# VectorE's order of work in the first two steps of a gated attention and feed-forward kernel

## The reference, cut to what matters

```python
x = x + tanh(g_xattn) * attention(layernorm(x), ctx_768, Wq, Wk, Wv, Wo, bo)
x = x + tanh(g_ffn) * ffn(layernorm(x), w_gate, w_up, w_down)

def ffn(x, w_gate, w_up, w_down):
    g = bitlinear(x, w_gate)                      # 512 -> 2048
    u = bitlinear(x, w_up)                        # 512 -> 2048
    h = square(relu(g)) * u
    return bitlinear(h, w_down)                   # 2048 -> 512

def bitlinear(x, w):    # act_quant: round(x * 127 / max|x|) by row; weight_quant: round(w / mean|w|) in -1..1
    return act_quant(x) @ weight_quant(w).T
```

## Time and profile before

| | |
|---|---|
| median of 3 runs | 1192.84 us (1191.83 to 1193.57) |
| profiled execution | 1192.0 us, its span 1190.1 us |
| PE busy | 1169.0 us, 98% |
| DVE busy | 1035.5 us, 87% |
| ACT busy | 869.1 us, 73% |
| POOL busy | 307.0 us, 26% |
| DMA queue q1 | 47.4% of 16 engines' span |

### The profile page before, as it was taken

How to read it: one execution, slowest core, us unless ns; L and a number is a source line. 1 busy time by engine, 2 the same in 40 slices (tenths; PEclk the granted TensorE clock), 3 DMA queues, 4 the chain that set the end, 5 groups by cost and what they waited for, 6 DMA issues and landing times.

```text
span 1190.1 us, 18790 instructions
## 1 busy us (share of the span) xinstructions
PE 1169.0 (98%) x5802; PEld 742.8 (62%) x5867; DVE 1035.5 (87%) x2124; ACT 869.1 (73%) x929; POOL 307.0 (26%) x313
## 2 busy tenths in 40 slices
PE   9989899999999999999999999999999999999998
PEld 7656556666665666666566656656665666666554
DVE  4989898888988888888998888888899888988887
ACT  4877777776886777677877767776787777677764
POOL 3222222222442222222442222222244222222200
PEclk9999999999999999999999999999999999999999
DMA  9792654443444464444444464443443444444333
GB/s 354 263 302 67 156 142 109 98 108 93 101 115 102 114 167 110 97 103 107 101 99 98 114 178 112 98 107 94 101 114 97 104 97 110 96 99 112 84 65 75
DMA packets 286484, 144.69 MB, mean 122 GB/s; under 512 B 254586, under 2 KB 255226, under 8 KB 283889
## 3 DMA queue, kind: packets, MB, share of 16 engines
q1 hardware_dynamic: 286445, 144.32, 47.4%
q10 hardware_dynamic: 4, 0.00, 0.0%
HBM read 57.86 MB, written 24.35 MB: 69 GB/s over the span
## 4 chain that ended last, share of the span: by engine, by line
PE 88%; DVE 4%; DMA 3%; ACT 3%; issue 2%; SPq 0%; POOL 0%; ACTq 0%; DVEq 0%; POOLq 0%
PE gu_ps L1084 34%; PE o_ps L1048 18%; PE y_ps L1098 17%; PE s_ps L66 17%; DMA v_scr<-x 1%; DMA w_down<-in_wu_t 1%; DVE staged L1324 1%; PE gu_ps L1148 1%; DVE half_max L1330 1%; DMA a_scr<-a_spare 1%; DVE w_down L1484 0%; ACT staged L730 0%; ACT x L762 0%; PE y_ps L1141 0%; ACT k_pairs L864 0%
## 5 line engine op out<-in xcount | busy, mean ns | idle before, releaser
L1084 PE MATMUL gu_ps<-w_up,xq_t 128*128 128x512 bf16 x1024 | 241.9, 379 | 0.7 <-DVE staged L1324 0.7
L1084 PE MATMUL gu_ps<-w_gate,xq_t 128*128 128x512 bf16 x951 | 226.3, 379 | 8.6 <-DMA xq_t<-xq 3.9
L1098 PE MATMUL y_ps<-w_down,hq_t 128*128 128x512 bf16 x1008 | 227.8, 379 | 0.0
L1048 PE MATMUL o_ps<-v_sb,pt_high 128*128 128x512 f32 (+1 forms) x640 | 212.8, 413 | 1.1 <-DVE pt_low L1313 1.1
L1324 DVE TENSOR_TENSOR staged<-staged,gu_ps 128x1024 f32<-128x1024 f32 x128 | 155.6, 1215 | 53.8 <-ACT staged L784 53.8
L66 PE MATMUL s_ps<-a_sb,xf_high 128*128 128x308 f32 x1024 | 187.3, 305 | 0.0
L1084 PEld LDWEIGHTS gu_ps<-w_up,xq_t 128*128 128x128 bf16 x1024 | 99.5, 98 | 122.8 <-DVE staged L1324 2.6
L645 POOL TENSOR_TENSOR rstd<-var_eps,neg_half 128x1 f32<-128x1 f32 x128 | 96.6, 755 | 307.9 <-DVE var_eps L1289 275.2
L824 ACT ACTIVATE staged<-staged,h_scale 128x1024 f32<-128x1024 f32 x126 | 137.9, 1141 | 48.7 <-DVE h_scale L1344 48.7
L1098 PEld LDWEIGHTS y_ps<-w_down,hq_t 128*128 128x128 bf16 x1008 | 97.8, 97 | 119.7
L778 ACT ACTIVATE staged<-gu_ps 128x1024 f32<-128x1024 f32 x127 | 128.9, 1015 | 53.9 <-PE gu_ps L1084 53.5
(11 more groups left out here) (146 smaller groups left out, 1439.7 us busy)
## 6 DMA issues: line engine op xcount, KB each, us to landing
xf_sb<-in_x_feat SPq DMA_DIRECT2D x64, 256.0 KB, 2.7
x_sb<-in_x_tok SPq DMA_DIRECT2D x64, 256.0 KB, 2.8
y<-staged SPq DMA_DIRECT2D x63, 256.0 KB, 2.0
staged<-in_wg_t SPq DMA_DIRECT2D x4, 1024.0 KB, 9.8
staged<-in_wd_t SPq DMA_DIRECT2D x4, 1024.0 KB, 7.5
folded<-a_scr SPq DMA_DIRECT2D x3, 1232.0 KB, 5.3
v_scr<-x SPq DMA_DIRECT2D x12, 256.0 KB
folded<-v_scr SPq DMA_DIRECT2D x3, 1024.0 KB, 5.0
```

The costliest lines, as they stand in the source:

```text
L1048: last = nc.tensor.matmul(o_ps[:, :], pt[0:rows, P * c:P * (c + 1)], v_sb[0:rows, v, c, :], start=(c == 0 and pt is pt_high and v == 0), s ...
L1084: last = nc.tensor.matmul(target[:, q, :], xq_t[:, s.par(0), c, :], w[:, c, cols], start=(c == 0), stop=(c == DC - 1))
L1098: last = nc.tensor.matmul(y_ps[:, :], hq_t[:, c, :], w_down[:, c, :], start=(c == 0), stop=(c == FC - 1))
```

## The change

In step 0, DVE's top_half(0), the maximum of the first hidden half, moves from directly behind hidden_half(0) to behind shift_scores, so that the input chain of tile 1 comes first. Step 1 gets a written order of its own. In it hidden_half(1) moves up to directly behind unmark_input; shift_scores follows; input_stats of tile 4 moves from ahead of top_scores to behind shift_scores; then top_half(0); probs_low of tile 3 is taken over from the beginning of step 2; hidden_unit_scale, top_half(1) and hidden_scales follow; sum_probs of tile 4 moves from ahead of hidden_half(1) to the very end. No instruction is added or taken away, and no other engine's program changes.

```diff
                 def first_step(s):
                     input_stats(s, 3)
                     hidden_half(s, 0)
-                    top_half(s, 0)
                     add_attention(s, 1)
                     input_scale(s, 1)
                     top_scores(s, 3)
                     unmark_input(s, 1)
                     shift_scores(s, 3)
+                    top_half(s, 0)
                     ternary(2, 2, w_down)
                     hidden_half(s, 1)
                     probs_low(s, 2)
...
+                def second_step(s):
+                    unmark_hidden(s, -1)
+                    hidden_half(s, 0)
+                    add_attention(s, 1)
+                    input_scale(s, 1)
+                    top_scores(s, 3)
+                    unmark_input(s, 1)
+                    hidden_half(s, 1)
+                    shift_scores(s, 3)
+                    input_stats(s, 3)
+                    top_half(s, 0)
+                    probs_low(s, 2)
+                    hidden_unit_scale(s, 1)
+                    top_half(s, 1)
+                    hidden_scales(s)
+                    sum_probs(s, 3)
+
                 def step(s):
                     if s.opens(0):
                         first_step(s)
                         return
-                    if s.has(1) and not s.opens(1) and s.has(3):
+                    if s.opens(1):
+                        second_step(s)
+                        return
+                    if s.has(1) and not s.opens(2) and s.has(3):
                         probs_low(s, 1)
...
-                    if s.has(3) and not s.opens(1):
+                    if s.has(3):
                         input_stats(s, 3)
...
-                    if s.opens(1):
-                        input_stats(s, 3)
```

## The result

The changed kernel takes 1197.16 us in the median of 6 runs (1195.0 to 1198.25), the kernel before, beside it, 1192.49 (1191.31 to 1194.35, 6 runs). The ratio is 1.0037, 95% interval 1.0024 to 1.005: 4.7 us slower at the median. The forecast was 1195.8, slower by 2.9 us, with a range from 1193.0 to 1197.2: the measured median lies at its very end. The profiled execution took 1196.87 us, its span is 1194.9 (before 1192.0 and 1190.1).

A forecast was written before the change was run, and what follows sets the result against it. PE is busy 98% of the span, paced early by the DVE and ACT ring with 0.33 us slack. Ring 3.27 us late less slack makes PE 2.94 late: 1192.84 + 2.94 = 1195.8 us, range 1193.0 to 1197.2.

The forecast's parts named there:

- Step 0: Input chain of tile 1: 1.13 us earlier without top_half(0), but DVE and PE's up product gain only 0.6 us.
- Step 1, the visible gain: PE, tiles 2 and 3: earlier input chain brings attention of tile 3 to 121.7 from 126.03; PE gains 4.4 us.
- Step 1, the tail: Late sum_probs delays normalise and planes of tile 4, so mark_hidden of tile 1 starts at 128.43, not 125.16: 3.27 us.
- no collision: Bound for probs_low beside POOL's xf_low: 0 us added before hidden_unit_scale instead of 0.3; time 0.3 us lower.
- full exclusion: DVE and POOL exclude each other at probs_low: 0.8 us added before hidden_unit_scale instead of 0.3; time 0.5 us higher.
- The ring: DVE and ACT loop from h_scale through mark_hidden, relu, square, hidden_half(0) to next h_scale: 16.87 us, forecast 3.27 late.
- One sign: PE, step 3: new idle before attention of tile 4, which starts at about 146.2 instead of 143.22.
- the sum: Whole kernel: median 1192.84 plus PE's 2.94 us delay at attention of tile 4 gives 1195.8 us.
- Rival 4: SP's transposes of tile 4's planes and tile 1's hidden halves crowd; a transfer 2 us late gives 1197.3; chance 0.10.
- the likeliest case's own range: Ring 2.77 to 4.37 us late, so PE 2.4 to 4.0 later: 1195.3 to 1196.9 us; chance 0.65.
- Rivals 1 to 3: PE's gain stays, 1188.4 us (0.08); mark_hidden not held by planes, 1192.0 (0.10); lag mostly dissolves, 1193 (0.07).

The follow-up runs named there:

- e1_step0_only: Kernel before with step 0's edit alone (top_half(0) moved behind shift_scores), step 1 as before; ratio to before 0.9992 (0.9984 to 1.0001).
- e6: Kernel before with one move, sum_probs of tile 4 to the end of step 1; ratio to before 1.0021 (1.0012 to 1.0029).
- e3: Changed kernel with sum_probs of tile 4 put back ahead of top_half(1); 1193.07 us against 1192.59 for the kernel before, ratio 1.0001.
- e4: Changed kernel with, on ACT in step 2 alone, mark_hidden of tile 1 ahead of part_probs of tile 4; ratio to before 1.0014 (1.0004 to 1.0024).
- after_again: The changed kernel itself, run and profiled again; 1196.22 us against 1192.93 for the kernel before, ratio 1.0038 (1.0023 to 1.0053).

## Why the prediction was right, and what it missed

**Step 0.** Forecast: everything on DVE 0.6 earlier, with bounds 0 and 0.8. Measured: ternary(2, 2) took 1.22 us instead of 1.86, and e1_step0_only moved mark by 0.76. The end of the input chain, unmark_input, at 97.14 (97.2 forecast), and PE's up product then waiting 0.46 for hidden_half(1), as said.

**Step 1, the visible gain.** Gate product of tile 2 at 118.25 (118.4), attention of tile 3 at 121.83 (121.7). Right, and as worthless as forecast.

**Step 1, the tail.** hidden_unit_scale at 122.22 (122.7 less 0.6); DVE waited for rstd 0.44, a little under the 0.5 to 1 forecast, because probs_low took up more of the time: its 1.51 us beside POOL's xf_low repeat the 1.57 of the earlier trace rows. With the 0.7 that step 0 really gave, the forecast's ends for this start were 121.7 (no collision) and 122.5 (full exclusion), so 122.22 lies between them. mark_hidden at 128.57 (128.43), with the wait changing from h_scale to planes. The ring was 3.3 to 3.4 late (3.27) and PE 2.97 to 3.02 late by it where the clock held (2.94). e6, e3 and e4 show this cause one by one. One sign failed in the first profile: PE was to stand ahead of the attention of tile 4, and it stood ahead of the gate product instead; in after_again it stands where forecast, 1.09 us.

**The step that was mis-sized** is the sum: it let PE wait 2.7 us in step 2 and again in step 3 at no price but the waiting. In the first profile 1.58 us came on top, from a late xq_t of tile 3 (4.2 us from issue instead of 2.4) and half clock in the product behind it, and the median was 4.7 us up, not 2.9 (3.3 in the second set of runs). The kernel before had stalls of 2.07 us here at full clock, so its rows gave no hint; e1_step0_only shows the same wait with the clock at half behind it. A bound could have been had from the product itself, 1.72 us on top if its time doubles (3.36 measured). Rival 4 had a late transfer of about that size, for other tiles, and saw only its wait, not the clock behind it. The wait for the hidden halves that it names came too (PE 0.91 us ahead of the down product in after_again) and was absorbed.

That the median lies inside the range is in part luck. It is 0.04 us below the range's end and 0.3 above the likeliest case's own range, which ends at 1196.9. The room above it was left for rival 4; no term of the sum stood for the clock, which filled part of it.

Rivals 1 to 3 are out: in no profile of the changed kernel was mark_hidden released by h_scale, and DVE's idle ahead of hidden_half(0) of tile 2 grew from 1.04 to 2.34 us instead of being filled.

## What to carry to other kernels

In a pipeline whose slowest engine is full, find the ring that releases it and measure the slack at the place where they meet (0.33 us by the rows of before, 0.36 by the table): a ring made late moves the end by its shift less that slack, and stalls of the full engine taken away upstream of that place are worth at most the slack. When an instruction is moved back, follow its product to the head of every in-order queue that it releases; what stands behind it there pays, though it never needed it. And give a new wait of TensorE one stretch at half clock on top, as the far end of the range: whether it comes, and whether it costs anything, differed between executions here.

## What the runs showed of the hardware

- The DMA that turns xq of tile 3 (128x512 bf16) landed 2.4 us after its issue in ten of the profiles, and 4.0 to 4.2 us after it in three (the first of the changed kernel, e3_sums_back, e4_mark_first), each of them with one packet of queue 8 (instructions, 0.02 MB) in the same stretch; none of the ten has one. That the packet causes the delay is read from this coincidence, not tested. Two profiles of one program differ in this.
- Behind PE's waits of 2.72 and 2.47 us the granted clock was at half in one profile of the changed kernel, the second time for the whole gate product of tile 3. In another, with waits of 2.72, 0.91 and 0.69 us, it stayed 1.00 throughout this stretch. In e1_step0_only it was at half behind 2.09 us, in the kernel before full behind 2.07 at the same place. So the length of the wait alone doesn't tell. With matmuls of no use in the waits it stayed 1.00 in one profile.
- VectorE's subtraction of two SBUF operands took 1.51 us beside GpSimd's subtraction and 0.82 alone. The GPSIMD Engine Reference of the Trainium skill, section 1 (Specifications), which says that such instructions contend with GpSimd, agrees. The other side pays as well: GpSimd's product took 1.69 us beside such a subtraction (e6_sums_last_only) and 1.22 alone.
